# A Perceiver block on one core: the query stage rebuilt, with layer norm scaling and Wk centring on GpSimd, query copies on VectorE, and batch 0's keys between the query tiles

## What is computed

```python
# layernorm: (x - mean) / sqrt(var + 1e-5), over the 512 features
q  = (layernorm(x) @ Wq)       # 8 heads of 64
kv = context @ Wkv             # k: first 512 columns, v: the others
q  = per_head_ln(q, qn_w)      # (q - mean over 64) * rsqrt(var + 1e-6) * w
k  = per_head_ln(k, kn_w)
attn = softmax(where(mask, q @ k.T * 64**-0.5, -inf))
x = x + (attn @ v) @ Wo
x = x + spiking_attention(layernorm(x), ...)
x = x + top2_experts(layernorm(x), ...)
```

## Time and profile before

| | |
|---|---|
| median of 3 runs | 844.58 us |
| the profiled execution | 846.15 us, span of the core 844.3 us |
| busy, share of the span | TensorE 88%, VectorE 64%, ScalarE 59%, GpSimd 31% |
| mean granted TensorE clock | 0.952 of full speed |
| query tiles | one each 4.75 us, tile 7's product ends at 50.16 us |
| scores of batch 0 | start at 74.56 us |

### The profile page before, as it was taken

How to read it: one execution, slowest core, us unless ns; L and a number is a source line. 1 busy time by engine, 2 the same in 40 slices (tenths; PEclk the granted TensorE clock), 3 DMA queues, 4 the chain that set the end, 5 groups by cost and what they waited for, 6 DMA issues and landing times.

```text
span 844.3 us, 13440 instructions
## 1 busy us (share of the span) xinstructions
PE 745.7 (88%) x4437; PEld 646.5 (77%) x4437; DVE 544.3 (64%) x1018; ACT 496.7 (59%) x1104; POOL 264.8 (31%) x178
## 2 busy tenths in 40 slices
PE   4787999999999999999999988899788828999960
PEld 3676999899898999999999967677577726888840
DVE  6946776776768868688677757734565563545522
ACT  3765776785767857678677654354265223565530
POOL 5253212121212212121212143635646212656530
PEclk9999999999999999999999999899898958999995
DMA  7933121221212121212122031230216652665658
GB/s 245 115 107 92 38 76 38 76 70 42 75 37 75 37 75 37 75 37 75 37 75 76 1 95 36 85 98 3 97 50 224 225 188 86 108 114 104 107 69 298
DMA packets 60024, 75.98 MB, mean 90 GB/s; under 512 B 8752, under 2 KB 33328, under 8 KB 59984
## 3 DMA queue, kind: packets, MB, share of 16 engines
q1 hardware_dynamic: 52528, 59.21, 23.4%
q0 software_dynamic: 5152, 12.06, 8.1%
q10 hardware_dynamic: 2304, 4.20, 1.4%
HBM read 54.75 MB, written 20.71 MB: 89 GB/s over the span
## 4 chain that ended last, share of the span: by engine, by line
PE 76%; DVE 9%; DMA 4%; ACT 4%; POOL 3%; issue 3%; SPq 0%; DVEq 0%; ACTq 0%; POOLq 0%
PE pK L32 35%; PE pV L32 12%; PE pP L32 10%; PE pS L32 5%; PE pT L1511 3%; PE pT L1360 3%; PE pP L1494 2%; DMA fin<-total 1%; DVE xn L894 1%; PE pT L1618 1%; DMA total<-big,idx 1%; DVE a_flat L1133 1%; DMA big<-x_rows,idx_x 1%; PE pS L1567 1%; DVE bst L884 1%
## 5 line engine op out<-in xcount | busy, mean ns | idle before, releaser
L32 PE MATMUL pK<-parts 128*128 128x512 f32 x864 | 221.3, 405 | 11.9 <-POOL parts L483 7.8
L32 PEld LDWEIGHTS pK<-parts 128*128 128x128 f32 x864 | 160.0, 192 | 43.2 <-POOL parts L483 8.2
L469 POOL TENSOR_TENSOR parts<-big,parts 128x1024 fp32r<-128x1024 f32 x32 | 77.4, 2418 | 344.8 <-ACT parts L651 344.8
L32 PE MATMUL pK<-w,lhs 128*128 x276 | 71.2, 408 | 1.3 <-DVE lhs L1288 1.1
L32 PEld LDWEIGHTS pK<-w,lhs 128*128 128x128 f32 x276 | 51.8, 194 | 12.9 <-issue 2.8
L1309 DVE TENSOR_TENSOR w_p<-big,w_p 128x1024 fp32r<-128x1024 f32 x23 | 28.2, 1226 | 51.4 <-ACT w_p L849 46.4
L926 DVE TENSOR_TENSOR kn<-pK,head_rs 128x512 f32<-128x512 f32 x64 | 44.0, 687 | 21.3 <-ACT head_rs L583 20.7
L32 PE MATMUL pS<-kT,qblk 128*128 128x258 f32 x384 | 51.4, 283 | 1.7 <-issue 1.7
L685 ACT ACTIVATE pT<-pP 128x512 fp32r<-128x512 f32 x32 | 19.1, 598 | 57.0 <-PE pP L1494 57.0
L32 PE MATMUL pP<-pT,parts 128*128 128x256 f32 x384 | 52.3, 285 | 0.0
L528 POOL DMA_INDIRECT total<-big,idx x23 | 36.4, 1585 | 44.7 <-ACT big L862 44.1
(11 more groups left out here) (243 smaller groups left out, 1587.6 us busy)
## 6 DMA issues: line engine op xcount, KB each, us to landing
big<-in_ctx_dram SPq DMA_DIRECT2D x32, 512.0 KB, 3.8
big<-in_L_ffn_w_dram SPq DMA_DIRECT2D x24, 512.0 KB, 4.8
total<-zero SPq DMA_DIRECT2D x32, 256.0 KB, 4.0
fin<-total SPq DMA_DIRECT2D x8, 512.0 KB, 7.8
big<-in_L_xattn_Wkv_dram SPq DMA_DIRECT2D x2, 1024.0 KB, 7.5
x_rows<-xn ACTq DMA_DIRECT2D x8, 256.0 KB, 2.3
total<-big ACTq DMA_DIRECT2D x8, 256.0 KB, 2.8
out_dram<-fin SPq DMA_DIRECT2D x4, 512.0 KB, 6.2
```

The source lines that it names most:

```text
L32: last = pe.matmul(out, lhs(a, c), rhs(b, c), start=start and c == first and n == 0, stop=stop and c == chunks - 1 and n == 2)
L469: nc.gpsimd.tensor_tensor(ctxN[:, u, LO], ctx_raw[:, u], ctxN[:, u, HI].bitcast(F32), ALU.subtract).then_inc(cn_lo, 1)
```

## The change

- **Layer norm scaling** (`ln_norm` of the first eight tiles) moves from VectorE to GpSimd; the statistics of tile n then wait for the scaling of tile n - 2, whose mean and root they overwrite.
- **Wk's centring** moves to GpSimd: VectorE sums all heads in tiles 0 and 1, scales the sums once, and GpSimd adds them.
- **Wq's low halves** 2 and 3 move from GpSimd to VectorE.
- **Query copies** move from ScalarE (4 of 128x128) to VectorE (1 of 128x512).
- **Order.** The layer norm runs two tiles ahead in place of one. The 257th keys' transposes stand behind tile 1, their product behind tile 4; batch 0's context transposes behind tiles 2 and 3, its key products behind tiles 5 and 6, into banks `pC` and work tiles `sq_x`, `kn_x` and a third column set of `head_ss`, `head_log`, `head_rs`. The queries of batches 0 and 1 are spread between the tiles. ScalarE copies Wk two chunks at a time in tiles 2 and 3, and Wv one chunk a tile in tiles 4 to 7.
- **Loads.** Three x tiles come first in place of two, Wq comes in two halves, the contexts ahead of the query scales, Wv behind them. Several semaphores are merged into `const_set` and `norm_in`; VectorE no longer waits for the identity matrix at its start.
- In `batch` what was moved is left out for batch 0.

The core of the diff, in the order SyncE, GpSimd, ScalarE, VectorE, TensorE:

```diff
-                    sp.wait_ge(w_lo[JOB[freed_by]], C)
+                    sp.wait_ge(w_lo[JOB[freed_by]], 2 if freed_by == "xq" else C)
                     sp.wait_ge(w_hi, high_count(freed_by, C - 1))
                 sp.dma_start(raw(name), jobs[name][0]).then_inc(raw_in(name)[0], 16)
...
-            sp.dma_start(x_all[:, 0:2, :], x_t[:, 0:2, :]).then_inc(x_in[0], 16)
-            load_weight("xq")
-            sp.dma_start(x_all[:, 2:TILES, :], x_t[:, 2:TILES, :]).then_inc(x_in[1], 16)
-            for i, (w, loaded) in enumerate(((qn_w, qn_in), (kn_w, kn_in))):
-                cols = w.rearrange("(c e) d -> (e d) c", c=C)
-                sp.dma_start(qk_col[:, i, :], cols, allow_slow_non_contiguous=True).then_inc(loaded, 16)
+            early = 3
+            sp.dma_start(x_all[:, 0:early, :], x_t[:, 0:early, :]).then_inc(x_in[0], 16)
+            sp.dma_start(raw("xq")[:, 0:2], jobs["xq"][0][:, 0:2]).then_inc(xq_half, 16)
+            sp.dma_start(raw("xq")[:, 2:C], jobs["xq"][0][:, 2:C]).then_inc(raw_in("xq")[0], 16)
+            sp.dma_start(x_all[:, early:TILES, :], x_t[:, early:TILES, :]).then_inc(x_in[1], 16)
             load_weight("xk")
-            sp.wait_ge(const_set, 1)
+            sp.wait_ge(const_set, 2)
             for r in range(3):
                 sp.dma_start(rem_raw[r * B:(r + 1) * B, :], ctx[:, M - 1, :]).then_inc(rem_in, 16)
-            load_weight("xv", "xq")
             for b in range(2):
                 sp.dma_start(ctx_raw[:, b], ctx[b, 0:MT * P, :].rearrange("(t p) d -> p t d", p=P)).then_inc(ctx_in[b], 16)
+            for i, w in enumerate((qn_w, kn_w)):
+                cols = w.rearrange("(c e) d -> (e d) c", c=C)
+                sp.dma_start(qk_col[:, i, :], cols, allow_slow_non_contiguous=True).then_inc(norm_in, 16)
+            sp.wait_ge(xq_lo, 2)
+            load_weight("xv", "xq")
             for g in range(HG):
                 sp.dma_start(masked[g * S:(g + 1) * S], mask.rearrange("b s m -> s b m")).then_inc(mask_in, 16)
...
-            for name in JOBS[:3]:
-                low_part(name)
+            def ln_norm(n):
+                pool.wait_ge(ln_rsd, n + 1)
+                if n >= 2:
+                    pool.wait_ge(ln_t, n - 1)
+                nc.gpsimd.tensor_scalar(ln_dst(n), x_all[:, n], mean_var[:, n % 2, 0:1], ln_rs[:, n % 2],
+                                        ALU.subtract, ALU.mult).then_inc(ln_x, 1)
+            def centre(name, c):
+                pool.wait_ge(w_sum, 2 * C + 1)
+                w = heads(raw(name)[:, c])
+                nc.gpsimd.tensor_tensor(w, w, per_head(head_mean[:, c]), ALU.add).then_inc(w_centred, 1)
+            pool.wait_ge(x_in[0], 16)
+            ln_norm(0)
+            ln_norm(1)
+            low_part("xq", (0, 1))
+            ln_norm(2)
+            pool.wait_ge(x_in[1], 16)
+            ln_norm(3)
+            ln_norm(4)
+            for c in range(C):
+                centre("xk", c)
+                if c == 1:
+                    ln_norm(5)
+            ln_norm(6)
+            low_part("xk", (0, 1))
+            ln_norm(7)
+            low_part("xk", (2, 3))
+            low_part("xv")
...
+            ln_high(0, lhs_p[:, 0, HI])
+            high_part("xq", (0, 1))
+            ln_root(2)
+            high_part("xq", (2, 3))
+            ln_high(1, lhs_p[:, 1, HI])
+            ln_root(3)
...
+            for t in range(TILES):
+                act.wait_ge(q_mm, t + 1)
+                if t >= 2:
+                    act.wait_ge(q_ss, t - 1)
+                act.activation(sq[:, t % 2], pKV[t % 2][:, :], ACT.Square).then_inc(q_sq, 1)
+                if t + 2 < TILES:
+                    ln_high(t + 2, lhs_p[:, t % 2, HI])
+                act.wait_ge(q_ss, t + 1)
+                act.activation(head_log[:, t % 2], head_ss[:, t % 2], ACT.Ln, bias=HEAD_B,
+                               scale=1.0 / HD).then_inc(q_lg, 1)
+                act.wait_ge(q_lg, t + 1)
+                if t >= 2:
+                    act.wait_ge(q_n, t - 1)
+                act.activation(head_rs[:, t % 2], head_log[:, t % 2], ACT.Exp, scale=-0.5).then_inc(q_rs, 1)
+                if t + 4 < TILES:
+                    ln_root(t + 4)
+                if t in (2, 3):
+                    high_part("xk", (2 * t - 4, 2 * t - 3))
+                if 4 <= t:
+                    high_part("xv", (t - 4,))
+                if t == 1:
+                    act.wait_ge(rem_pe, 1)
+                    act.activation(remT[:, HI], pAV[0], ACT.Copy).then_inc(rem_act, 1)
+                if t in (2, 3):
+                    act.wait_ge(ctx_t, t - 1)
+                    act.activation(ctxT[:, 0, HI, :, (t - 2) * P:(t - 1) * P], pAV[3 - t], ACT.Copy).then_inc(ctx_hi, 1)
+                if t == 4:
+                    act.wait_ge(rem_pe, 2)
+                    act.activation(sq_x[:, :], pV1[:, :], ACT.Square).then_inc(rem_act, 1)
+                    act.wait_ge(rem_dve, 2)
+                    act.activation(head_log[:, 2], head_ss[:, 2], ACT.Ln, bias=HEAD_B, scale=1.0 / HD).then_inc(rem_act, 1)
...
+                if t in (5, 6):
+                    n = t - 5
+                    if n == 0:
+                        act.activation(ctxN[:, 0, HI], ctx_raw[:, 0], ACT.Copy).then_inc(cn_hi, 1)
+                    act.wait_ge(k_mm, n + 1)
+                    act.activation(sq_x[:, :], pC[1 - n], ACT.Square).then_inc(k_sq, 1)
+                    if n == 0:
+                        act.wait_ge(q_out, 1)
+                        query_high(0, 0)
+                    act.wait_ge(k_ss, n + 1)
...
+                if t == 6:
+                    query_high(1, 1)
...
+                if 2 <= n < TILES:
+                    dve.wait_ge(ln_x, n - 1)
...
-                dve.wait_ge(*raw_in(name))
+                dve.wait_ge(*((xq_half, 16) if name == "xq" and c < 2 else raw_in(name)))
...
-            dve.wait_ge(const_set, 2)
-            nc.vector.tensor_reduce(sel[:, :], ident[:, 0:3 * B].rearrange("p (j b) -> p b j", j=3), AX.X, ALU.add).then_inc(sel_set, 1)
...
+            for c in (2, 3):
+                dve.wait_ge(w_hi, high_count("xq", c))
+                tt(w_slot[:, 0, LO, c], raw("xq")[:, c], w_slot[:, 0, HI, c].bitcast(F32), ALU.subtract).then_inc(xq_lo, 1)
+            ln_low(1, lhs_p[:, 1, LO], lhs_p[:, 1, HI])
+            dve.wait_ge(x_in[1], 16)
+            ln_stats(3, x_all[:, 3])
+            def query_out(t):
+                dve.wait_ge(q_t, t + 1)
+                tt(qoT[:, :, t * P:(t + 1) * P], pS[:, t % 2, :].rearrange("p (c n) -> p c n", c=C),
+                   qk_col[:, 2, :].unsqueeze(2).broadcast_to([P, C, P]), ALU.mult).then_inc(q_out, 1)
...
+            for t in range(TILES):
+                dve.wait_ge(q_sq, t + 1)
+                nc.vector.tensor_reduce(head_ss[:, t % 2], heads(sq[:, t % 2]), AX.X, ALU.add).then_inc(q_ss, 1)
+                if t + 2 < TILES:
+                    ln_low(t + 2, lhs_p[:, t % 2, LO], lhs_p[:, t % 2, HI])
+                dve.wait_ge(q_rs, t + 1)
+                if t >= 2:
+                    dve.wait_ge(q_t, t - 1)
+                tt(heads(kn[:, t % 2]), heads(pKV[t % 2][:, :]), per_head(head_rs[:, t % 2]),
+                   ALU.mult).then_inc(q_n, 1)
+                if t + 4 < TILES:
+                    ln_stats(t + 4, x_all[:, t + 4])
+                if t < 2:
+                    for c in (2 * t, 2 * t + 1):
+                        head_sums("xk", c)
+                if t == 1:
+                    dve.wait_ge(w_sum, 2 * C)
+                    ts(head_mean[:, :, :], head_mean[:, :, :], -1.0 / HD, None, ALU.mult).then_inc(w_sum, 1)
+                    dve.wait_ge(norm_in, 32)
+                    stt(qk_col[:, 2, :], qk_col[:, 0, :], SCALE, qk_col[:, 1, :], ALU.mult, ALU.mult).then_inc(qk_set, 1)
+                    dve.wait_ge(qk_set, 1)
+                if t >= 1:
+                    query_out(t - 1)
+                if t == 1:
                     dve.wait_ge(rem_act, 1)
                     tt(remT[:, LO], pAV[0], remT[:, HI].bitcast(F32), ALU.subtract).then_inc(rem_dve, 1)
...
+                if t in (2, 3):
+                    dve.wait_ge(ctx_hi, t - 1)
+                    part = slice((t - 2) * P, (t - 1) * P)
+                    tt(ctxT[:, 0, LO, :, part], pAV[3 - t], ctxT[:, 0, HI, :, part].bitcast(F32),
+                       ALU.subtract).then_inc(ctx_lo, 1)
+                if t == 4:
+                    dve.wait_ge(rem_act, 2)
+                    nc.vector.tensor_reduce(head_ss[:, 2], heads(sq_x[:, :]), AX.X, ALU.add).then_inc(rem_dve, 1)
+                    dve.wait_ge(const_set, 4)
+                    nc.vector.tensor_reduce(sel[:, :], ident[:, 0:3 * B].rearrange("p (j b) -> p b j", j=3), AX.X, ALU.add).then_inc(sel_set, 1)
+                    dve.wait_ge(rem_act, 4)
+                    tt(heads(kn_x[:, 2]), heads(pV1[:, :]), per_head(head_rs[:, 2]), ALU.mult).then_inc(rem_dve, 1)
+                if t in (5, 6):
```

(90 more changed lines are left out.)

157 lines of the change are left out of this document (29 added, 128 removed).

## The result

The changed kernel takes 852.23 us (median of 5 runs, 851.21 to 855.42) against 844.58 of the kernel before on the same chip (841.74 to 846.67): a ratio of 1.0095, interval 1.0064 to 1.0126. It is slower, as forecast, but by 7.7 us instead of 4.5, and 0.7 above the range. The changed kernel once more (experiment 1) gave 851.77 against 843.53: 1.0098, interval 1.0077 to 1.0120. The profiled execution took 851.21 with a span of 849.5.

What follows compares the result with a forecast made beforehand. VectorE was taken to bound the query stage, TensorE the rest from 76 us. T 1.3 us later plus two slow clocks of 1.6 gave +4.5 us, 849.1; 8-in-10 range 842.5 to 851.5.

Steps and rivals of the forecast that it cites:

- T: Start of batch 2's context transposes on TensorE; forecast at 77.4 us against 76.1 at full clock, released by that context's load.
- The other road: From tile 7's product through batch 0's scores to T; forecast shorter than the load's, 12.1 us, at 71.
- Rival 3: At T: the saving arrives whole, no wait for the load, T at 72; -4 us, 840.6; chance 0.08.
- The tiles: Query stage: chains of waits make tile 0 take 3.9 us, tiles 1 and 2 5.7 each, tile 3 alike.
- R0 to R3: Starts of VectorE's sums of tiles 0 to 3; forecast at 18.9, 22.8, 28.5 and 34.2 us.
- Rival 2: At S: no wait, T at 73.8 to 71.6; from -0.7 to -4.5 us, down to 840.1; chance 0.20.
- S: End of Wk's last low half on GpSimd, awaited by the 257th keys' product; forecast 40.8 us, TensorE idling 3.6.
- rival 4: At the start: GpSimd's low half 1 waits behind VectorE's low halves, ending 1.5 us later; +6.0, 850.6; chance 0.10.
- Layer norm scaling on GpSimd: Each moved scaling priced at 0.6 us, bounds 0.44 and 1.3; later ones claimed to lie in GpSimd's idle time.
- The start: First tile's product forecast to end at 18.3 us against 18.9, gaining only 0.6; its sum starts at 18.9.
- The clock: TensorE's clock falls to 0.50 after idling, slowing work at S and at T; +1.6 us each.
- Rival 1: One slow clock only, S keeping the full one; +2.9 us, 847.5; chance 0.22.

Runs made afterwards that it cites:

- Experiment 2: Changed kernel with GpSimd's mask inversion and small constants moved in front of Wv's low halves: 845.48 us, ratio 1.0028.
- experiment 5: Kernel before the change, with the mask inversion and constants moved in front of Wv's low halves: 843.28 us, ratio 0.9994.
- experiment 6: Kernel before the change, with six more GpSimd operations, results unused, behind Wq's low halves to price one-input operations: one execution, 842.32 us.
- experiment 3: Changed kernel with all eight layer norm scalings back on VectorE: 854.58 us, ratio 1.0133.
- 12: Changed kernel with early mask, 257th keys' product behind tile 5's, tile 7's scaling behind Wk's low halves, first two scalings on VectorE: 837.46 us, ratio 0.9910.
- experiment 9: Changed kernel with GpSimd's layer norm scaling of tile 7 moved behind all of Wk's low halves: 850.38 us, ratio 1.0068.
- experiment 7: Changed kernel with twenty extra TensorE matmuls, results overwritten, before the wait for Wk's low halves: 850.82 us, ratio 1.0089.
- 8: Changed kernel with twenty extra matmuls before the wait for Wk's low halves and eight more behind batch 0's scores: 849.04 us, ratio 1.0072.
- 11: Changed kernel with early mask inversion, 257th keys' product behind tile 5's, and tile 7's scaling behind Wk's low halves: 837.76 us, ratio 0.9925.
- 10: Changed kernel with mask inversion ahead of Wv's low halves and the 257th keys' product behind tile 5's product: 842.52 us, ratio 0.9978.
- 4: Changed kernel with all layer norm scalings back on VectorE and the mask inversion ahead of Wv's low halves: 846.50 us, ratio 1.0034.

## Why the prediction was right in direction and short in size

**What sets T: right.** The forecast had T released by the load, and its chain from tile 7's product: 2.5 + 16.1 = 18.6. Measured: 64.83 to 83.40, 18.6. (The old 50.16, to which the prediction compares tile 7's product, is the start of its Square, which stood behind another copy on ScalarE; the product ended at 49.94. No term of the sum uses it.) The other road, through the scores, took 15.1 instead of 12.1 (scores done at 79.96) and stayed hidden behind the load. Experiment 2 takes 6.3 us away by moving only the mask, and experiment 5 shows that the same move gives nothing where the slack is. Rival 3, the saving arriving whole, is out.

**The tiles: right.** The sums R0 to R3 are 4.05, 5.52 and 5.53 apart where 3.9, 5.7 and 5.7 were forecast. Rival 2, no wait at S, is out: TensorE idles 5.47 there. At the start VectorE's centrings went ahead of GpSimd's second low half, as forecast, and not VectorE's own low halves, so rival 4 is out too.

**The step that failed: "Layer norm scaling on GpSimd".** I took 0.6 and called 1.3 the upper bound. It takes 2.08 (and 3.03 for tile 2's, at 16.12, beside VectorE's own low halves). I priced a float32 operation from the mask inversion, which works on bytes (0.86 ns an element); experiment 6 gives 3.4 to 4.1 for float32. The upper bound was no bound either: it assumed that one input can't cost more than two. From this term follow two misses of place. The start: the statistics wait for the first scaling, and product 0 ends at 20.41 instead of 18.3, 2.1 late. VectorE waits 1.58 for it, where 0.6 would have left hardly any wait. How much of the 2.1 it makes is not shown in full: with the first two scalings on VectorE (experiments 3 and 12), which then makes them itself, the first product starts 0.5 earlier. And S: I had the later scalings "in GpSimd's idle time", but GpSimd has none from 29.42 to 45.87; S is R3 + 8.6 instead of R3 + 6.6, and experiment 9 puts it back at R3 + 6.6 (36.06 and 42.67) by moving one scaling. There ScalarE's copies of Wk are the next bound, which is why taking all scalings off GpSimd (experiment 3) gives nothing more.

**The sum again.** With the slow clock at S my T was 77.4 + 1.6 = 79.0. Add 2.1 for the start, 2.0 for S, 0.5 for the stretch from S to tile 7 (20.07 instead of 18.0 + 1.6; the slow product took 5.01 against the 4.58 that I had), and take off 0.1 for the tiles and the step into them: 83.5, measured 83.40.

**The clock: right, and slightly larger.** The 257th keys' product took 5.01 at the granted 0.50, and 3.07 when TensorE was kept busy before it (experiment 7): 1.9 to 2.0 for the forecast 1.6, and 2.4 in the traces that have 5.46. Behind T the delay grows from 7.1 (76.26 to 83.40) to 8.9, so 1.8 for 1.6. Rival 1, one slow clock only, is out: both are in the trace, and experiments 7 and 8 remove one after the other there (with a new short one from 66 to 69 us, see the last section).

**What stays open.** The first product of probabilities is 8.9 later, the two profiled spans differ by 5.2, and the medians by 7.7. Single executions of one kernel lie 5 us apart, so the 8.9 and the 7.7 can't be told apart by it. That scatter lies behind the stage: from the first product of probabilities to the end of the span thirteen profiled executions (all but experiment 6) take 752 to 759 us, in no order that follows the edits, though the work there is the same. Nor is it shown why versions 11 and 12 gain 6.8 and 7.1 where T is 3.8 and 5.6 earlier; intervals of plus or minus 2.5 us cover the second gap and just miss the first. Experiment 3 leaves open what a full return of the scalings would cost in a better queue order; only one order was tried. And whether the load of the next Wq behind that of batch 2's context would bring T down to its scores in experiments 10 to 12 is untested.

## What to carry to other kernels

Price an operation that the trace lacks from a row of the same element type, and don't take the two-input row for a ceiling of the one-input one; if the price is disputed and decides the sum, let it range to several times the row. When work moves to an idle engine, write out that engine's queue for the stretch: here it is not the 31% share that counts but the 15 us without a gap in front of one low half. And before counting a saving, walk from the moved work's last link to the next load: a long operation that nobody is waiting for (the mask inversion) belongs in front of the late short one (Wv's last chunk), and a product that waits for much belongs behind the one that is ready. When a load moves, look at what is issued just ahead of it.

## What the hardware showed that I had not expected

- A float32 operation with one input takes longer on GpSimd (2.08 to 2.26 us for 128x512 with two per-partition scalars) than one with two inputs (1.28 to 1.41 in the kernel before); with two constants it takes 1.91 where as many bytes take 0.62.
- A VectorE operation on 128x8 elements between two tiles in SBUF, 0.17 us before, took 2.35 us in the changed kernel, from 73.64 to just behind the end of GpSimd's mask inversion at 75.62, and held batch 0's scores until 77.04. In experiment 3 a scaling on VectorE grew from 0.53 to 1.21 beside GpSimd's centring of Wk and to 1.54 beside a low half. The wait at 73.64 was covered, since T waited longer for the load. The Trainium skill (SBUF — State Buffer, section "SBUF: two separate sides") says that GpSimd's instructions and those of VectorE that read two operands from SBUF or run in a 2-port mode share a port pair, and that whichever starts first holds it for its whole instruction. The trace agrees, if this operation is one of those, and shows that even so small a one is held.
- TensorE idled 5.47 us and was granted 0.50 behind it; after 0.76 to 0.79 of idling (experiments 7, 8 and 11), with work in front, it kept the full clock. The length of the wait alone does not tell which: after the same 2.27 us of idling behind tile 7's product the clock stayed at 1.00 in the changed kernel (67 to 69 us) and fell to 0.50 in experiments 7 and 8 (67 to 68 us), whose transposes there took 1.77 and 1.91 instead of 1.04. Why is open.
- The load of batch 2's context (512 KB) took 3.6 to 3.9 us from issue to landing in the changed kernel and experiments 1, 3, 7, 8 and 9, and 6.4 to 7.9 where a 1 MB load had been issued 2.5 to 2.6 us ahead of it (experiments 2, 4, 10, 11 and 12).
